# Start-up of an attention and feed-forward kernel: later loads of x, and G, E, V of batch 1 ahead of P of batch 0

## The reference, cut to what matters

```python
z(W, b) = x + x @ W.T + b              # q, k1, k2, v1, v2, split into 16 heads of 8
S1 = k1^T v1 / n ;  S2 = k2^T v2 / n   # per batch and head, 8 x 8
out = q@S1 * mean(v2) * g1 + sum(S1*S2) * g2 + q@S2 * mean(v1) * g3 + q@(S1*S2) * g4
out = layernorm(out) * ln_g + ln_b ;  attn = out @ Wo.T + bo
x1 = layernorm(x + attn)
y  = layernorm(x1 + relu(x1 @ w1 + b1) @ w2 + b2) * gamma + beta
result = layernorm(x1 + y)
```

## Time and profile before

| | us |
|---|---|
| median of 3 runs | 215.61 (215.06 to 217.07) |
| the profiled execution, whole | 217.56 |
| its span, first to last instruction | 215.8 |
| PE busy in the span | 195.8 (91%) |
| DVE, ACT, POOL busy | 163.6, 127.5, 136.4 |

### The profile page before, as it was taken

The page is one execution under the profiler, slowest core; times in us unless marked ns, Lnnn a source line. Parts: engine busy times, 40 slices in busy tenths (PEclk is TensorE's granted clock), DMA queues, the critical chain, the costliest instruction groups (busy, mean ns, idle before and its releaser), DMA issues.

```text
span 215.8 us, 4250 instructions
## 1 busy us (share of the span) xinstructions
PE 195.8 (91%) x1377; PEld 178.0 (82%) x1377; DVE 163.6 (76%) x478; ACT 127.5 (59%) x383; POOL 136.4 (63%) x177
## 2 busy tenths in 40 slices
PE   7959999999998999899989999899989999899930
PEld 7858998988997879787979999798979998888630
DVE  0272854989777986989688886898688877896895
ACT  0332439364659575766577565947576557867571
POOL 8804551464896659675966589655967397766230
PEclk9979999999999999999999999999999999999996
DMA  5999500000010100110010001010011001011012
GB/s 150 241 211 290 133 0 5 2 0 5 0 49 0 52 2 0 53 49 0 0 52 16 34 3 49 2 52 0 2 49 53 0 0 52 0 50 49 3 50 97
DMA packets 12116, 9.98 MB, mean 46 GB/s; under 512 B 727, under 2 KB 9950, under 8 KB 12094
## 3 DMA queue, kind: packets, MB, share of 16 engines
q1 hardware_dynamic: 11056, 8.52, 12.7%
q0 software_dynamic: 448, 0.92, 2.2%
q10 hardware_dynamic: 590, 0.26, 0.6%
HBM read 5.51 MB, written 4.19 MB: 45 GB/s over the span
## 4 chain that ended last, share of the span: by engine, by line
PE 51%; DVE 19%; ACT 13%; issue 8%; DMA 3%; POOL 3%; DVEq 0%; ACTq 0%; POOLq 0%
PE down_ps L901 17%; PE up_ps L901 13%; PE prep_ps L901 11%; PE z_ps L901 6%; DVE st L700 5%; ACT res L580 5%; DMA late_rows<-in_L_ffn_b 3%; DVE y2n L705 3%; DVE x1T_lo L837 3%; ACT hT L597 2%; PE turn_ps L1028 2%; ACT z_sq L558 2%; ACT x1T_hi L647 2%; DVE z_ps L799 2%; PE turn_ps L999 2%
## 5 line engine op out<-in xcount | busy, mean ns | idle before, releaser
L901 PE MATMUL down_ps<-w_sb,hT 128*128 128x128 f32 x496 | 61.1, 277 | 0.1
L901 PEld LDWEIGHTS down_ps<-w_sb,hT 128*128 128x128 f32 x496 | 58.4, 192 | 1.2 <-DVE y2n L705 0.4
L597 ACT ACTIVATE hT<-up_ps,cols 128x512 f32<-128x512 f32 x64 | 41.5, 682 | 3.6 <-PE up_ps L901 3.5
L509 POOL TENSOR_TENSOR x1b<-x,b_rows 128x512 f32<-128x512 f32 x16 | 20.6, 1287 | 19.1 <-DVE x L705 19.1
L901 PE MATMUL up_ps<-x1T_hi,w_hi 128*128 128x512 f32 x64 | 26.5, 414 | 4.7 <-ACT hT L597 4.7
L483 POOL TENSOR_TENSOR y2g<-y2n,gamma_rows 128x512 f32<-128x512 f32 x14 | 17.9, 1280 | 13.4 <-DVE y2n L705 13.4
L580 ACT ACTIVATE res<-y,nb,rstd 128x128 f32<-128x128 f32 x60 | 24.6, 482 | 2.1 <-POOL nb L471 2.1
L901 PE MATMUL up_ps<-x1T_lo,w_hi 128*128 128x512 f32 x64 | 25.5, 398 | 0.0
L901 PE MATMUL up_ps<-x1T_hi,w_lo 128*128 128x512 f32 x64 | 25.3, 396 | 0.0
L558 ACT ACTIVATE z_sq<-z_ps 128x128 f32<-128x128 f32 x64 | 16.9, 272 | 12.3 <-PE z_ps L901 12.2
L498 POOL TENSOR_TENSOR xu<-X,u_rows 128x512 f32<-128x512 f32 x16 | 19.0, 1189 | 5.5 <-DVE u_rows L696 5.5
(11 more groups left out here) (151 smaller groups left out, 429.6 us busy)
## 6 DMA issues: line engine op xcount, KB each, us to landing
X<-in_L_attn_x SPq DMA_DIRECT2D x8, 512.0 KB, 9.8
out<-res SPq DMA_DIRECT2D x15, 256.0 KB, 2.0
w_sb<-in_L_ffn_w POOLq DMA_DIRECT2D x2, 256.0 KB, 9.6
out<-res SPq DMA_DIRECT2D x2, 128.0 KB, 1.9
w_raw<-in_L_attn_Wv ACTq DMA_DIRECT2D x2, 64.0 KB, 2.8
w_raw<-in_L_attn_Wk SPq DMA_DIRECT2D x2, 64.0 KB, 4.1
bv_rows<-in_L_attn_bv ACTq DMA_DIRECT2D x2, 64.0 KB, 6.1
g_row<-in_L_attn_g ACTq DMA_DIRECT2D x4, 0.1 KB
```

What stands on the lines that cost most here:

```text
L509: pool.tensor_tensor(x1b2[(s + 1) % 2][:, :, :], x1[:, :, :], rows(b2_rows[:, :]), ALU.add).then_inc(x1b2_out, 1)
L597: act.activation(hT[:, k, :], up_ps[k % len(up_ps)][:, :], ACT.Relu, bias=cols[:, 5 + k:6 + k]).then_inc(relu_out, 1)
L901: return pe.matmul(o, lhsT, rhs, start=start, stop=stop)
```

## The change

It has these parts. SP issues the late vectors (ln_g, ln_b, b1) right behind Wk1 and Wk2, which POOL no longer does, then waits until the small vectors and bv have landed, and only then issues x of batches 1 to 7. On PE, `keep_warm(3)` (writing `up_ps` bank 0) stands between `turn_late` and `ak_e(0)`; `gram_av(1)` moves ahead of `attention_matrix(0)`; `ak_e(1)` moves from the middle of `product(0, 0)` to right behind `centered(0)`. S of batch 1 goes to `up_ps` bank 1 in place of `prep_ps`, and `gram(3)`, which uses that bank, waits for `s_out(1)`. On DVE, E and V of batch 1 come ahead of `xT_rest(0)` and `s_out(1)` right behind `PQ_rest(0)`, so ahead of `split_w1`.

```diff
+        def s_bank(b):
+            return up_ps[1] if b == 1 else prep_ps
...
-                                                in1=prep_ps[:, j * 128:(j + 1) * 128],
+                                                in1=s_bank(b)[:, j * 128:(j + 1) * 128],
...
             for i, w in enumerate((Wk1, Wk2)):
                 sp.dma_start(w_raw[:, 2 + i, :], w[:, :]).then_inc(kv_loaded, 16)
+            for i, v in enumerate((ln_g, ln_b)):
+                sp.dma_start(late_rows[i:i + 1, :], row(v)).then_inc(late_loaded, 16)
+            sp.dma_start(late_rows[2:6, :], b1[0, :].rearrange("(k c) -> k c", c=128)).then_inc(late_loaded, 16)
+            sp.wait_ge(vec_loaded, VECTORS)
+            sp.wait_ge(bv_loaded, 16 * 2)
             for b in range(1, BATCHES):
                 load_x(b)
...
-            for i, v in enumerate((ln_g, ln_b)):
-                pool.dma_start(late_rows[i:i + 1, :], row(v)).then_inc(late_loaded, 16)
-            pool.dma_start(late_rows[2:6, :], b1[0, :].rearrange("(k c) -> k c", c=128)).then_inc(late_loaded, 16)
...
+            def e_and_v(b):
...
-                if st.prep:
...
+                if st.prep and st.n != -1:
+                    e_and_v(st.prepared())
...
-                if st.prep and st.n != -2:
+                if st.prep and st.n >= 0:
                     s_out(dve, st.prepared())
                 if st.n == -2:
                     prepare(dve, 0)
                     u_row()
+                    e_and_v(1)
                     xT_rest(0)
                     PQ_rest(0)
+                    s_out(dve, 1)
...
             def keep_warm(times):
                 for _ in range(times):
-                    mm(down_ps[:, 0:128], ident[:, :], ident[:, :])
+                    mm(up_ps[0][:, 0:128], ident[:, :], ident[:, :])
...
             def gram(b, tiles):
                 pe.wait_ge(x_loaded[b], 16)
+                if b == 3:
+                    pe.wait_ge(S_out, 2)
...
-                    last = mm(prep_ps[:, j * 128:(j + 1) * 128], A_kv[:, 3 + j, :], E_sb[:, j, :])
+                    last = mm(s_bank(b)[:, j * 128:(j + 1) * 128], A_kv[:, 3 + j, :], E_sb[:, j, :])
...
                     turn_late()
+                    keep_warm(3)
                     ak_e(0)
                     output_rows()
                     gram(1, range(SEQ_TILES))
+                    gram_av(1)
                     attention_matrix(0)
                     centered(0)
+                    ak_e(1)
                     return
                 if st.n == -1:
-                    gram_av(1)
                     gram(2, range(0, 3))
-                    product(0, 0, lambda: ak_e(1))
+                    product(0, 0)
                     turn_x(1)
```

More of the change, by code:

```diff
@@ L750, in add_y2 @@
                                   x1b2[s % 2][:, :, :], ALU.add).then_inc(y2_out, 1)
+            def e_and_v(b):
+                wait(dve, ev_done, b + 1)
+                wait(dve, s_done, b)
+                wait(dve, M_out, b * 2)
+                if b == 0:
+                    dve.wait_ge(bv_loaded, 16 * 2)
+                dve.scalar_tensor_tensor(out=E_sb[:, :, :].rearrange("p j c -> p (j c)"),
+                                         in0=bv_rows[:, 0:2, :].rearrange("p j c -> p (j c)"),
+                                         scalar=G_sb[:, b, C:C + 1], in1=ev_bank(b)[:, 0:256],
+                                         op0=ALU.mult, op1=ALU.add)
+                if b == 0:
+                    dve.wait_ge(nbv_ready, 1)
+                dve.tensor_tensor(V_sb[:, :, :].rearrange("p j c -> p (j c)"), ev_bank(b)[:, 256:512],
+                                  nbv_rows[:, :, :].rearrange("p j c -> p (j c)"), ALU.add).then_inc(EV_out, 1)
             def body(st):
@@ L760, in body @@
                     normalize(y2n, y2_tile, st3, rstd3, y2n_out)
-                if st.prep:
-                    b = st.prepared()
-                    wait(dve, ev_done, b + 1)
-                    wait(dve, s_done, b)
-                    wait(dve, M_out, b * 2)
-                    if b == 0:
-                        dve.wait_ge(bv_loaded, 16 * 2)
-                    dve.scalar_tensor_tensor(out=E_sb[:, :, :].rearrange("p j c -> p (j c)"),
-                                             in0=bv_rows[:, 0:2, :].rearrange("p j c -> p (j c)"),
-                                             scalar=G_sb[:, b, C:C + 1], in1=ev_bank(b)[:, 0:256],
-                                             op0=ALU.mult, op1=ALU.add)
-                    if b == 0:
-                        dve.wait_ge(nbv_ready, 1)
-                    dve.tensor_tensor(V_sb[:, :, :].rearrange("p j c -> p (j c)"), ev_bank(b)[:, 256:512],
-                                      nbv_rows[:, :, :].rearrange("p j c -> p (j c)"), ALU.add).then_inc(EV_out, 1)
+                if st.prep and st.n != -1:
+                    e_and_v(st.prepared())
                 if st.n == -2:
```

## The result

The changed kernel takes 222.19 us (median of 4 runs, 220.55 to 222.69), the kernel before 215.51 (4 runs, 215.06 to 217.07): the ratio is 1.026, 95% interval 1.020 to 1.032. The forecast was 213.5, 1% faster, with a range of 212.6 to 215.2; it came out about 3% slower, outside the range. The profiled execution took 222.38 with a span of 220.6, so here the profile stands at its kernel's median.

A forecast was written before the change was run, and what follows sets the result against it. PE bounds the steady part, so only the start-up until product(1, 0) could change. Terms 1.48 + 1.29 - 1.41 + 0.68 + 0.10 = 2.14 took the median from 215.61 to 213.5, range 212.6 to 215.2.

The forecast's parts named there:

- part 2: Start-up loads: x of batches 1 to 7 held until bv lands at 8.2; E starts 1.30 earlier, x of batch 1 lands at 13.2.
- the lower bound: Load of x of batch 1, issued at 8.2: at best 3.5 us from issue, landing at 11.7.
- the 3.2 that the prediction worked out from the page: Load of x of batch 1: fixed 2.0 us plus bytes at 436 GB/s, estimated 3.2 us, landing at 11.4; not used.
- part 1: Start-up: late vectors on SP's queue remove PE's whole wait for them; POOL's other seven DMAs start about 1.5 us sooner.
- rival (b): Before gram(1): bv lands at 10.7 to 11.9, x of batch 1 late, clock falls; 1.7 slower, 217.3; chance 0.08.
- The breakeven, 15.5: Landing of x of batch 1 (13.36 + 2.14) from which on rival (b) decides.
- the five terms: Start-up until product(1, 0): 1.48 + 1.29 - 1.41 + 0.68 + 0.10 = 2.14 us won.
- the 1.29 of the clock: PE from output_rows to attention_matrix(0): 3.68 us becomes 2.39 at full clock, 1.29 won.
- the 1.48 (late vectors and bv): Start-up to output_rows: 1.30 from V earlier plus 0.18 from late columns not waiting; 14.34 becomes 12.86.
- 1.41 for `gram_av(1)` and its wait: PE ahead of attention_matrix(0): 0.55 wait for ACT's copy of G plus 0.86 for gram_av(1), 1.41 lost.
- 0.68 back from the product: Middle of product(0, 0), with ak_e(1) and its wait moved out: 2.23 becomes 1.55, 0.68 won before turn_x(1).
- Rival (a): Start-up: the clock falls all the same, 3.4 us stay at 1.2 GHz; gain only 1.0, 214.6; chance 0.14.

The follow-up runs named there:

- the quiet run: The change with its hold-back, POOL issuing bo, b2, beta, gamma, w1 and w2 only when x of batch 1 has landed: 217.67 us, ratio 1.008 to the kernel before.
- the second profile: The kernel before, unchanged, run again to profile its start-up: the profiled execution took 215.14 us; median of its ten runs 216.99, ratio 1.001.
- the run in which x landed at 15.2: The change, with POOL too waiting for bv before it issues bo, b2, beta, gamma, w1 and w2: 218.71 us, ratio 1.011 to the kernel before.

## Why the prediction was wrong

**The step that failed** is in part 2: "At 5.2 us as x of batch 0 it lands at 13.4 ... I take 13.2, for by then POOL's loads are mostly through." It landed at 18.1. Two terms were too small. bv was taken to land at 8.2, and landed at 10.0; 8.0 to 8.4 is what it does with POOL's loads out of the way too, so the x loads were rightly seen as a cause, and POOL's were priced at too little. And x of batch 1 took 8.04 us from issue to landing where I had 5.2; it takes 4.0 with none of POOL's loads beside it, 5.3 beside w1 and w2, 6.9 to 8.0 beside all of them. (The 3.5 of the lower bound and the 3.2 that the prediction worked out from the page are below anything that the runs show; and POOL's "other seven DMAs" of part 1 are six.) And the half clock behind the wait, which the forecast's own sum did not have, cost 2 us more. The argument against rival (b), 2.4 MB at 0.24 MB per us, failed because POOL's loads did not move at that rate: the stretches of 9 to 11 us in the changed kernel have busy engines and few bytes.
```profile
9.00:10.00 1.00, 1.00 (x5) 0.84 (x6) 0.28 (x2) 0.00 (x0) 0.56 (x1) 1.00 1.43 74
10.00:11.00 1.00, 1.00 (x9) 0.81 (x8) 0.88 (x4) 0.95 (x3) 0.51 (x1) 1.00 0.75 21
```
The last two columns are the share of the engines and GB/s: 0.75 of 16 engines for 21 GB/s. A rate from a stretch of x loads was applied to another sort of load.

That fits the time up to 13 us. The queues of the changed kernel (packets, MB, share of 16 engines) from 12 to 13, and from 13 to 18:
```profile
q0 software_dynamic: 26, 0.10, 26.9%
...
q1 hardware_dynamic: 2151, 1.09, 89.3%
q0 software_dynamic: 135, 0.39, 20.2%
```
SP's queue, q1, has no packet at all in the three microseconds from 10 to 13, though x of batch 1 was issued at 10.08; in the quiet run its first packet stands 1.4 us behind the issue. A packet counts whole in the microsecond where it starts, so the stretches belong together: from 9 to 13 the shares are 1.43, 0.75, 1.11 and 0.27, in all 3.56 of 4 us, for 74, 21, 102 and 98 GB/s. From 13 on the engines move 295 GB/s, and q1 moves 1.09 MB, twice x of batch 1, before that load has landed at 18.11: x of batches 2 and 3, issued at 10.67 and 11.38, travel with it, and w1 and w2 beside them. So two pieces make the 8.0 us: some 3 us in which POOL's slow packets fill most of the engines' time, and some 5 us at a high rate that other loads share. How much of the second piece is batches 2 and 3 was not tried: no run issues x of batch 1 behind bv and holds the later batches until it has landed.

**Rival (b)** had the outcome, place and clock included, with a chance of 0.08 and a price of 1.7 us. Its way there was another: bv at 10.7 to 11.9 and x of batch 1 in the same 5.2 us, where the profile has 10.0 and 8.0. So it shares the failed step, and its price was too low: it put x at 15.9 to 17.1 and 0.5 to 1.3 for the clock; the runs show 18.1 and 2.0. The breakeven, 15.5, is not borne out: the run in which x landed at 15.2 was already 1.1% slower than before. It had been worked out against a start-up that most runs don't have.

**The baseline.** The sum was made against a profile 1.95 us above its kernel's median, and I carried the difference through as if it lay outside the start-up. It lay in it. Of the five terms the 1.29 of the clock is in the first profile of before alone, and the 1.48 (late vectors and bv) shrinks: against the second profile `output_rows` came 13.26 - 12.19 = 1.07 sooner, and the clock had nothing to give. So even with x on time the change could only win 1.07 - 1.41 + 0.70 + 0.16 = 0.5 us; the run with its order and bv ahead of x shows 215.48 against 215.64, none that can be told.

**What was right.** The order's cost: 1.41 for `gram_av(1)` and its wait, 0.68 back from the product. With equal loads (bv on SP's queue) and full clock, `gram(1)` to `attention_matrix(0)` takes 15.05 - 13.16 = 1.89 in the old order and 16.50 - 13.10 = 3.40 in the new, 1.51 more where 1.41 was forecast; and `attention_matrix(0)` to `turn_x(1)` is 28.95 - 23.64 = 5.31 in the change and 6.01 in the second profile of before, 0.70 less. `s_out(1)` right behind the fix and the wait of `gram(3)` cost nothing (no idle time ahead of either). The steady part carries a shift one to one: the start of `product(1, 0)` moved from 28.73 to 35.94, 7.21 us, and the time from 215.14 to 222.38, 7.24.

Those 7.21 us in their parts, from the two timelines: `gram(1)` starts 18.16 - 13.78 = 4.38 later. From there to `attention_matrix(0)` it is 5.48 where it was 1.79, 3.69 more (1.87 of it the slower `gram(1)`, the rest the wait for the copy and `gram_av(1)`, itself partly at half clock). To `turn_x(1)` 0.70 less, to `product(1, 0)` 0.16 less.

Rival (a), a clock that falls all the same, did not come about as such: in the profiles with x on time and the late vectors on SP the clock was at 1.00 from 12 to 25 us. In the change it fell through the wait of (b). In the two profiles of before the clock and the landings differ together, so how much of the spread of the runs is the clock's own was not tried.

**Open.** Why the change without its waits (217.5 over its seven runs below 220) is 1.3 slower than the same order with the loads of before (216.26) was not settled: in the first POOL's rows start 1.5 us sooner and the late vectors stand on another queue, and no run parts these two. Why x of batch 1 takes 8.4 us behind bv on SP's queue even with three of the rows gone is open too.

## What to carry to other kernels

Before a load is held back until another has landed, price its own landing from issue at the new time with what other queues do then, not from a quiet row; and where the wanted load can stand ahead of it in the same queue, that costs the issuing engine no wait (here 0.5% faster in place of 2.6% slower). When a profile lies outside the narrow group of its kernel's runs, take a second one or ask what is in it that the others lack: a wait that only some executions have cannot be won in the median. A wait on PE can cost itself and then the half clock of what follows, which here was 2 us on a wait of 5.3; behind one wait of 1.96 the clock was still at 1.00 (POOL waiting for bv), behind one of 1.94 it was at 0.50 from 21 to 23 us (only w1 and w2 beside x of batch 1).

## What the runs showed of the hardware that I had not expected

Loads that spread a row of 512 bytes over 128 partitions keep DMA engines busy while little is moved: from 10 to 11 us in the changed kernel, when b2, beta and gamma were in flight (landed at 11.1, 11.9 and 13.7; w1 and w2 stood behind them in the queue), 11 packets of POOL's queue took 74.6% of 16 engines and 21 GB/s were moved. Six of the eleven carry less than 512 bytes; if the time is the other five's, it is 0.746 x 16 / 5 = 2.4 us each. The rows of that microsecond:
```profile
DMA packets 11, 0.02 MB, mean 21 GB/s; under 512 B 6, under 2 KB 6, under 8 KB 11
...
q0 software_dynamic: 11, 0.02, 74.6%
```
And a 512 KB load of x took 4.0 us from issue to landing with none of POOL's loads beside it, 5.3 with w1 and w2, 6.9 to 8.0 with all six, each of these one execution.
